# Products of ones in two stages, a split search in a third, joined halves in a fourth: one change to a four-layer decoder kernel

## The reference

```python
# layer 1, self attention (16 heads of 8): two inner gradient steps of a linear model
Z = k @ W0;  dz1 = vjp(LN, Z)(LN(Z) - v)
Z2 = Z - (mask * k k^T) @ dz1;  dz2 = vjp(LN, Z2)(LN(Z2) - v)
ctx = q @ W0 - (mask * q k^T) @ (dz1 + dz2)      # group norm over tokens, then Wout
# layer 1, cross attention (2 heads of 64) over latents and masked context,
#   RMS-normed q and k; then the router of the next feed-forward part
# layer 2, cross attention and modulation: scores masked to each row's 32 largest
#   of 120, softmax, mean over 4 heads, film = c @ W_film + b_film, x scaled and shifted
# layer 3, cross attention (16 heads of 8): softmax((x q_w + q_b)(c k_w + k_b)^T / sqrt(8)) @ v
x = x + _L3_xattn_ref(_layernorm(x, axis=-1), ctx_768, L3_xattn_q_w, ...)
```

## Time and profile before

| | |
|---|---|
| median of 3 runs | 4454.17 us (4453.13 to 4456.05) |
| profiled execution | 4449.1 us, span 4447.3 us |
| TensorE busy | 3383.5 us, 76% |
| VectorE busy | 2825.5 us, 64% |
| ScalarE busy | 1819.8 us, 41% |
| GpSimd busy | 680.4 us, 15% |
| mean granted clock of TensorE | 0.819 |

### The profile page before, as it was taken

How to read it: one execution, slowest core, us unless ns; L and a number is a source line. 1 busy time by engine, 2 the same in 40 slices (tenths; PEclk the granted TensorE clock), 3 DMA queues, 4 the chain that set the end, 5 groups by cost and what they waited for, 6 DMA issues and landing times. The chain is left out here.

```text
span 4447.3 us, 71062 instructions
## 1 busy us (share of the span) xinstructions
PE 3383.5 (76%) x21887; PEld 2428.7 (55%) x21951; DVE 2825.5 (64%) x8344; ACT 1819.8 (41%) x5244; POOL 680.4 (15%) x867
## 2 busy tenths in 40 slices
PE   3668379366665885756888867999969997996887
PEld 3546279122223663544556754666657776554777
DVE  6556633599995874365885443444457776566997
ACT  1356234111113663213775333222235554445886
POOL 0044523000003775201000110000000000000000
PEclk9889589566666665577777777999989998998999
DMA  4030167100004000513000000000000000000000
GB/s 115 1 164 0 36 209 234 50 0 0 0 0 154 1 0 18 150 52 90 0 0 0 1 10 0 10 9 9 0 20 0 0 0 3 1 0 15 1 0 19
DMA packets 111454, 152.52 MB, mean 34 GB/s; under 512 B 21594, under 2 KB 88216, under 8 KB 109718
## 3 DMA queue, kind: packets, MB, share of 16 engines
q1 hardware_dynamic: 99822, 142.12, 10.3%
q0 software_dynamic: 11520, 9.05, 0.7%
HBM read 107.45 MB, written 58.50 MB: 37 GB/s over the span
## 5 line engine op out<-in xcount | busy, mean ns | idle before, releaser
L1260 PE MATMUL l_attn_p_s<-l_attn_outer,l_attn_upper 128*128 128x512 f32 x256 | 204.3, 972 | 113.9 <-DVE l_attn_outer L1203 100.0
L95 POOL TENSOR_TENSOR rstd<-vareps,minus_half 128x32 f32<-128x32 f32 x11 | 59.8, 5438 | 1455.7 <-DVE vareps L86 1322.5
L398 ACT ACTIVATE l_ffn_sg<-l_ffn_p_g 112x512 f32<-112x512 f32 x192 | 114.6, 597 | 391.8 <-PE l_ffn_p_g L378 371.9
L409 DVE TENSOR_TENSOR l_ffn_h<-l_ffn_sg,l_ffn_p_u 112x512 f32<-112x512 f32 x192 | 131.8, 687 | 172.6 <-PE l_ffn_p_u L381 172.0
L381 PE MATMUL l_ffn_p_u<-l_ffn_f_xTall,l_ffn_wu 128*112 x384 | 199.1, 600 | 7.3 <-DVE l_ffn_h L409 7.3
L1418 POOL DMA_INDIRECT slots_in<-l_xattn_x,l_xattn_slot x192 | 190.1, 990 | 81.9 <-issue 50.4
L378 PE MATMUL l_ffn_p_g<-l_ffn_f_xTall,l_ffn_wg 128*112 x384 | 199.0, 600 | 0.9 <-DVE l_ffn_al L2450 0.9
L1260 PEld LDWEIGHTS l_attn_p_s<-l_attn_outer,l_attn_upper 128*128 128x128 f32 x256 | 79.2, 324 | 218.6 <-issue 174.2
L387 PEld LDWEIGHTS l_ffn_p_o<-l_ffn_wd,l_ffn_h 112*128 112x128 f32 x1536 | 176.6, 192 | 15.7 <-issue 15.7
L2614 ACT ACTIVATE l_attn_E<-l_attn_p_s,l_attn_nm 128x128 f32<-128x128 f32 x512 | 180.9, 385 | 2.9 <-DVE l_attn_nm L2572 2.9
L387 PE MATMUL l_ffn_p_o<-l_ffn_wd,l_ffn_h 112*128 112x128 f32 x1536 | 176.7, 275 | 0.0
(11 more groups left out here) (790 smaller groups left out, 9505.8 us busy)
## 6 DMA issues: line engine op xcount, KB each, us to landing
l_experts_w<-in_L_ffn_w SPq DMA_DIRECT2D x72, 512.0 KB
slots_in<-l_xattn_empty SPq DMA_DIRECT2D x8, 2145.0 KB, 24.0
shares_out<-l_xattn_zero SPq DMA_DIRECT2D x24, 512.0 KB, 12.5
l_combine_got<-shares_out SPq DMA_DIRECT2D x16, 768.0 KB, 4.5
l_attn_toep<-kernel_rows SPq DMA_DIRECT2D x1, 8192.0 KB, 31.6
xattn_toep<-ssm_rows SPq DMA_DIRECT2D x1, 8192.0 KB
l_slots_w<-in_L_ffn_w SPq DMA_DIRECT2D x32, 176.0 KB
l_experts_x<-slots_in SPq DMA_DIRECT2D x72, 65.0 KB
```

The costliest lines, as they stand in the source:

```text
L398: act.activation(X.sg[:, k % 2], X.p_g[0:X.FP, k % 2], ACT.Silu).then_inc(s.silu_ready, 1)
L409: dve.tensor_tensor(X.h[:, k // X.FC, k % X.FC], X.sg[:, k % 2], X.p_u[0:X.FP, k % 2], ALU.mult).then_inc(s.h_ready, 1)
L1260: mm = pe.matmul(p_s[:, r, a], upper[:], outer[:, r, a * 512:(a + 1) * 512], start=True, stop=True)
```

## The change

Four edits, one per stage, and constants for them.

1. `kept_warm` issues n products of a 128 x 128 block of ones (bf16) with 512 columns of ones, into a bank that is not in use. `l1_attn` has 10 of them ahead of the wait for outer2, 4 ahead of the wait for ctx_ready and 4 ahead of the wait for squares_ready in each slot; `l1_xattn` has 1 behind the transposes of E and 2 behind the transpose of the normed row.
2. `l2_film`: the bias of the film, 1 row in f32, becomes 3 rows in bf16 (three parts that add up to the f32 value), cut ahead of the loop.
3. `l2_film`: the search is done as rounds 0 and 1 of tile t - 1, then item 3 (xin), then rounds 2 and 3.
4. `l3_xattn`: the halves are joined (one maximum, one exponential, one wait for all scores), and the third product takes the transposed maximum with a fixed picking matrix: 16 products of 128 columns where there were 4 of 512; VectorE's nmB becomes a copy.

```diff
+def kept_warm(R, pe, bank, n):
+    for _ in range(n):
+        pe.matmul(bank, R.onesb[:], R.onesb[:].unsqueeze(1).broadcast_to((P, 4, P)), start=True, stop=True)
...
# l1_attn, tensor
                     for b, u in item(2):
+                        for c, _ in item(1):
+                            pe.wait_ge(s.xT_ready, c + 1)
+                        kept_warm(R, pe, p_t[:], 10)
                         for r in range(2):
                             for c, _ in item(1):
                                 pe.wait_ge(s.proj_read, c * 2 + (r + 1))
...
                     for b, u in item(3):
+                        kept_warm(R, pe, p_c[:], 4)
                         pe.wait_ge(s.ctx_ready, b + 1)
...
                     for b, u in item(2):
+                        for c, _ in item(0):
+                            kept_warm(R, pe, p_t[:], 4)
                         pe.wait_ge(s.squares_ready, b + 1)
...
# l1_xattn, tensor
                         mm.then_inc(s.eT_psum, 1)
+                        kept_warm(R, pe, p_s[:, 0], 1)
                     for b, u in item(5):
                         pe.wait_ge(s.xhat_ready, b + 1)
                         for new, _ in item(2):
                             pe.wait_ge(s.qkT_ready, new + 1)
                         pe.transpose(p_n[:, 376:376 + P], xh[:, u % 2], R.ident[:]).then_inc(s.xhatT_psum, 1)
+                    for b, u in item(3):
+                        kept_warm(R, pe, p_s[:, 0], 2)
...
# l2_film, vector, ahead of the loop
-                last.then_inc(s.set_ready, 1)
+                chain(last)
+                for r in range(3):
+                    whole = bf[0:3] if r == 0 else brest[:]
+                    chain(dve.tensor_copy(bpart[:], whole))
+                    if r == 0:
+                        chain(dve.tensor_scalar(bparts[:], bpart[:], R.ident[0:3, 0:1], None, ALU.mult))
+                    else:
+                        last = dve.scalar_tensor_tensor(out=bparts[:], in0=bpart[:], scalar=R.ident[0:3, r:r + 1], in1=bparts[:],
+                                                        op0=ALU.mult, op1=ALU.add)
...
+                    chain(dve.tensor_tensor(brest[:], whole, bpart[:], ALU.subtract))
+                def searched(u, rounds):
+                    for r in rounds:
...
# l2_film, vector, in the loop, under item(1)
-                        for r in range(TOP // 8):
...
+                        searched(u, (0, 1))
                     for b, u in item(3):
                         dve.wait_ge(s.film_done, b + 1)
                         chain(dve.tensor_tensor(f[:], xr[:, u % 2], p_f[:, 0:P], ALU.mult))
                         dve.tensor_tensor(row(xin, b), f[:], p_f[:, P:256], ALU.add).then_inc(s.xin_done, 1)
+                    for b, u in item(1):
+                        searched(u, (2, 3))
...
# l2_film, tensor
-                    pe.matmul(out[:, 0:256], R.ones[0:1, :], bf[0:1, cols], start=True, stop=False)
+                    pe.matmul(out[:, 0:256], ones3[:], bparts[:, cols], start=True, stop=False)
...
# l3_xattn, vector
+                dve.tensor_copy(pick[:], slot4[:].unsqueeze(2).broadcast_to((P, SUB, SC)))
...
-                        for r in range(2):
-                            dve.wait_ge(s.scores_psum, b * 2 + (r + 1))
-                            last = dve.tensor_reduce(nm[:].rearrange("p (j r) -> p j r", j=4)[:, 2 * r:2 * r + 2, 0:SUB],
-                                                     p_s[:, 2 * r:2 * r + 2, 0:SUB * SC].rearrange("p j (m k) -> p j m k", m=SUB), AX.X, ALU.max, negate=True)
-                        last.then_inc(s.max_ready, 1)
+                        dve.wait_ge(s.scores_psum, b + 1)
+                        dve.tensor_reduce(nm[:].rearrange("p (j r) -> p j r", j=4)[:, :, 0:SUB],
+                                          p_s[:, :, 0:SUB * SC].rearrange("p j (m k) -> p j m k", m=SUB), AX.X, ALU.max, negate=True).then_inc(s.max_ready, 1)
...
-                        dve.tensor_tensor(nmB[:], p_c[:, P:256].unsqueeze(1).broadcast_to((P, SUB, P)),
-                                          slot4[:].unsqueeze(2).broadcast_to((P, SUB, P)), ALU.mult).then_inc(s.shift_spread, 1)
+                        dve.tensor_copy(nmT[:], p_c[:, P:256]).then_inc(s.shift_spread, 1)
...
# l3_xattn, scalar
-                        for r in range(2):
-                            act.activation(E[0:SC, 2 * r:2 * r + 2], p_s[0:SC, 2 * r:2 * r + 2], ACT.Exp).then_inc(s.exp_ready, 1)
+                        act.activation(E[0:SC], p_s[0:SC], ACT.Exp).then_inc(s.exp_ready, 1)
...
# l3_xattn, tensor
+                        after(pe, s.exp_ready, b)
                         for j in range(4):
-                            if j % 2 == 0:
-                                after(pe, s.exp_ready, b * 2 - 1 + j // 2)
...
-                        for j in range(4):
-                            rows = slice(32 * j, 32 * j + 32)
-                            mm = pe.matmul(p_s[0:SC, j], R.ones[rows, 0:SC], nmB[rows].rearrange("p m t -> p (m t)"), start=False, stop=True)
+                        for m in range(SUB):
+                            for j in range(4):
+                                rows = slice(32 * j, 32 * j + 32)
+                                mm = pe.matmul(p_s[0:SC, j, m * P:(m + 1) * P], pick[rows, m], nmT[rows], start=False, stop=(m == SUB - 1))
```

More of the change, by code:

```diff
@@ L2101, in _ @@
                 dve.tensor_copy(onesb[:], R.ones[0:1, :])
+                dve.tensor_copy(ones3[:], R.ones[0:3, :])
                 dve.wait_ge(s.rstd_ready, 1)
@@ L2119, in _ @@
                     last = dve.tensor_tensor(t[:, 0:P], t[:, 0:P], gam[:], ALU.mult)
-                last.then_inc(s.set_ready, 1)
+                chain(last)
[7 more added lines that the diff above has]
+                                                        op0=ALU.mult, op1=ALU.add)
+                        if r == 2:
+                            last.then_inc(s.set_ready, 1)
+                            break
+                        chain(last)
+                    chain(dve.tensor_tensor(brest[:], whole, bpart[:], ALU.subtract))
+                def searched(u, rounds):
+                    for r in rounds:
+                        src = sc[:, u % 2] if r == 0 else wk[:]
+                        for h in range(H):
+                            last = dve.max(top[:, h, 8 * r:8 * r + 8], src[:, h])
+                        if r == TOP // 8 - 1:
+                            last.then_inc(s.top_ready, 1)
+                            break
+                        chain(last)
+                        if r == 0:
+                            dve.tensor_scalar(nm[:], top[:, :, 0], -1.0, None, ALU.mult).then_inc(s.max_ready, 1)
+                        for h in range(H):
+                            last = dve.match_replace(wk[:, h], top[:, h, 8 * r:8 * r + 8], src[:, h], -3e38)
+                        chain(last)
                 for item in skewed(dve, 3):
```

23 lines of the change are left out of this document (7 added, 16 removed).

## The result

| | before | after |
|---|---|---|
| median, on the same chip | 4456.04 us (4446.47 to 4464.94, 12 runs) | 4466.81 us (4460.26 to 4472.39, 12 runs) |
| profiled execution | 4449.1 us | 4462.27 us, span 4460.5 us |
| mean granted clock | 0.819 | 0.845 |

The ratio of the times is 1.0025, 95% interval 1.0017 to 1.0033. The change makes the kernel 0.25% slower; the forecast was 4431 us, faster by 0.5%. TensorE's mean clock rose, and the time rose with it.

A forecast was written before the change was run, and what follows sets the result against it. No touched stage was full of one engine alone; VectorE set l1_attn's slot, l3_xattn was a chain. 4449.1 - 12 + 0 - 22 + 11 = 4426.1, plus 5.1 for the median: 4431 us, range 4423 to 4440.

The forecast's parts named there:

- The four terms: Predicted changes by stage: l1_attn -12 us, l1_xattn 0, l2_film -22 and l3_xattn +11.
- What they may give is the clock of the group at 1074.52: l1_attn: ones speed eight f32 records, 6.58 us now, 3.3 at 2.4 GHz; 0.85 us gained 14 times, -12 us.
- rival 1: l1_attn: the ones don't raise the clock where it counts, so the stage gives 0; 4443 us, chance 0.14.
- the gain is a share of a small thing and the loss needs 1.2 GHz at one place, so I take 0: l1_xattn: gain at most -6 us, loss +13 if the ones before the router product run slow; taken as 0.
- The last sign of being wrong: l1_xattn: the forecast is wrong if the ones' records are followed late by the router product.
- The bound of +13: l1_xattn: ones at 1.2 GHz before the router product cost 0.4 us in each of 32 slots, +13 us.
- a clock well above 0.65: l1_xattn: expected sign of the forecast holding, with the slot unchanged within 0.2 us.
- Slot: 9.15 + 0.3 = 9.45: l2_film: 9.15 us of work plus a 0.3 us reciprocal wait, against 10.24 before; -24.5 us over 31 slots.
- that part gets 0.8 + 1.8 us: l2_film: TensorE's part of the slot gets 0.8 us shorter and begins up to 1.8 us earlier; argued against rival 3.
- Rival 3: l2_film: the gain doesn't come, as ScalarE's sums stay late; 4453 us, no difference, chance 0.08.
- The sum of steps: l3_xattn: estimated steps after joining put the transpose 0.33 us later per slot, slots near 8.4 us, stage +11.
- rival 4: l3_xattn: joined halves serialise; if score products also queue, stage +38 us, kernel slower at 4459 us, chance 0.07.

The follow-up runs named there:

- attn_four: The kernel before with only the four products of ones ahead of ctx_ready in l1_attn; ratio 0.9980.
- x_row: The kernel before with l1_xattn's 1 + 2 products of ones, each 1 row deep instead of full; ratio 1.0002.
- x_ones: The kernel before with l1_xattn's 1 + 2 full products of ones alone; ratio 1.0027, 12 us.
- x_more: The kernel before with 2 + 4 full products of ones in l1_xattn in place of 1 + 2; ratio 1.0080, 36 us.

## Why the prediction was wrong

The four terms were -12, 0, -22 and +11 us, in sum -23; the whole measured +11. The parts measured -8 (l1_attn, by its times; -14 by its traces), +12 (l1_xattn), -10 (l2_film, by its trace) and +16 (l3_xattn), which add up to +10, or +4 with the -14. The spread of l1_xattn from one execution to the next, up to 8 us, is as large as what is left between these.

*l1_attn: right in mechanism.* "What they may give is the clock of the group at 1074.52" came out: 3.70 us in half of the slots and about 5.4 in the others instead of 6.58, VectorE's p_s wait gone, 2.7 us more of a wait for p_o in its place, direct cost 0. That four of the products stand in the pause after which the clock falls was in rival 1's "against"; that these four do all of it, attn_four shows. The size, -12, lies between the traces (-14) and the times (-8).

*l1_xattn: the step that failed* is "the gain is a share of a small thing and the loss needs 1.2 GHz at one place, so I take 0". The loss did need 1.2 GHz at that place, and x_row shows that without it there is none. I took the clock at that place as given, from the rows of before, when the ones themselves decide it: with full ones the fast part of the slot is no longer where they stand but behind them (x_ones), and the place costs 0.65 us more from E's transposes to the router product (2.40 against 1.75), of which the median slot with a fast part shows 0.36 (10.66 against 10.3). The last sign of being wrong, the router product late behind the ones, is the one that came. The bound of +13, worked out from that case, held for the times (12 us); the trace, at +19.4, lies outside. The sign "a clock well above 0.65" was a false friend: 0.69 in the changed kernel, 0.73 in x_ones, 0.80 in x_more, each slower than the last.

The Trainium skill, "TensorE: Matmul & The Clock Gate", Part 1, says that the gate follows how busy the array has been. If busy means the busy time of the trace, these runs don't agree: 307.65 us busy of 335 went with a clock of 0.65 and 280.35 us with 0.73. What differed in the kernels was how many rows the products used.

*l2_film: the step that failed* is "Slot: 9.15 + 0.3 = 9.45", applied to all 31 slots. TensorE's wait for xin went and the wait at the reciprocal came in each slot, as written. But the quick slot is 9.61: 0.34 more between mask and reciprocal and about 0.1 more in the divided search. And "that part gets 0.8 + 1.8 us" was not enough for the slots with a slow part, which are 10.17 and 10.48. 0.16 x 31 = 5 and (9.80 - 9.61) x 31 = 6 are the 11 of the missing 12 us. Rival 3 (ScalarE's sums stay late) was half true. That the edits have no gain singly was in none of my cases: I had added a gain for each.

*l3_xattn: right in mechanism, short in size.* The sum of steps gave 8.36 and the slot is 8.57. The release of the scores after E took 0.14 us where I wrote 0.05, and the other four steps were 0.02 to 0.05 longer each: 0.21 x 31 = 6.5 us. The score products don't serialise, so rival 4 didn't happen; the kernel got slower by another way than the one I had given a chance of 0.07.

The three misses (12, 12 and 5 us) have one sign and with the 4 of l1_attn's times make 33 of the 34 us. Two of them are about TensorE's clock in places that I had read off the trace of before and held fixed.
